# Expert groups of an attention and mixture-of-experts layer: opening products of two experts in a row, then closing products of two

## What is computed

```
x: (32, 256, 128) f32           # 8192 tokens of 128 channels
x = layernorm(x + attention(x)) # 16 heads of 8
# mixture of experts on the result xf, 8192 x 128
scores = sigmoid(xf @ gate_w.T)
sel    = top_k(scores + expert_bias, 2)
for e in range(8):              # each token goes to two experts
    h     = silu((s*xf) @ w1[e].T) * ((s*xf) @ w3[e].T)
    out_r = h @ w2[e].T         # kept where expert e was chosen
shared = silu(xf @ sw1.T) * (xf @ sw3.T) @ sw2.T
x = layernorm(x + shared + s * out_r)
```

## Time and profile before

| | |
|---|---|
| median of 3 runs | 772.97 us (772.28 to 772.98) |
| profiled execution, whole time | 773.07 us |
| profiled execution, span of the records | 771.3 us |
| attention phase, up to the first opening product | 426.6 us |
| expert phase, first opening product to the end | 344.7 us |
| busy in the span: PE, PEld, DVE, ACT, POOL | 744.4, 532.1, 635.0, 520.8, 501.8 us |

### The profile page before, as it was taken

How to read it: one execution, slowest core, us unless ns; L and a number is a source line. 1 busy time by engine, 2 the same in 40 slices (tenths; PEclk the granted TensorE clock), 3 DMA queues, 4 the chain that set the end, 5 groups by cost and what they waited for, 6 DMA issues and landing times.

```text
span 771.3 us, 20493 instructions
## 1 busy us (share of the span) xinstructions
PE 744.4 (97%) x7004; PEld 532.1 (69%) x7004; DVE 635.0 (82%) x1358; ACT 520.8 (68%) x1067; POOL 501.8 (65%) x715
## 2 busy tenths in 40 slices
PE   4899999999999999999998899999999999999996
PEld 2255656566566565665554688888888888888886
DVE  7789999999999999999998557888667666666676
ACT  2178899998889898898888546445455454545442
POOL 5546788887787877878634556566656556555564
PEclk9999999999999999999999999999999999999999
DMA  4747766676565665656610645555554655454540
GB/s 115 200 134 189 183 169 178 187 185 176 151 164 166 174 176 160 157 167 162 172 38 23 196 121 111 121 132 128 141 123 126 130 130 127 125 128 120 125 111 28
DMA packets 202336, 108.92 MB, mean 141 GB/s; under 512 B 10504, under 2 KB 202248, under 8 KB 202248
## 3 DMA queue, kind: packets, MB, share of 16 engines
q1 hardware_dynamic: 199792, 105.75, 53.0%
q10 hardware_dynamic: 2456, 2.05, 1.0%
HBM read 73.41 MB, written 33.82 MB: 139 GB/s over the span
## 4 chain that ended last, share of the span: by engine, by line
PE 92%; DVE 4%; DMA 2%; issue 1%; ACT 1%; SPq 0%; POOL 0%; POOLq 0%; DVEq 0%; ACTq 0%
PE bank L952 16%; PE bank L762 16%; PE bank L734 11%; PE bank L769 9%; PE bank L770 8%; PE bank L771 8%; PE bank L747 8%; PE bank L851 3%; PE bank L825 2%; PE bank L873 2%; PE bank L905 1%; PE bank L880 1%; DVE negmax L1101 1%; PE bank L790 1%; PE bank L889 1%
## 5 line engine op out<-in xcount | busy, mean ns | idle before, releaser
L1101 DVE TENSOR_REDUCE negmax<-bank 128x2 f32<-128x512 f32 x512 | 322.9, 678 | 18.5 <-PE bank L747 16.1
L598 ACT ACTIVATE probs<-bank 128x512 f32<-128x512 f32 x512 | 294.2, 613 | 48.2 <-PE bank L734 44.3
L708 ACT ACTIVATE q_stack<-k_stack 128x512 f32<-128x512 f32 x128 | 80.8, 631 | 152.2 <-DVE k_stack L1160 152.1
L747 PE MATMUL bank<-k_stack,q_stack 48*128 48x256 bf16 x1024 | 163.8, 281 | 3.7 <-DVE negmax L1101 2.3
L734 PE MATMUL bank<-q_stack,k_stack 50*128 50x256 bf16 x1024 | 157.9, 275 | 0.8 <-ACT probs L598 0.7
L1160 DVE TENSOR_TENSOR k_stack<-bank,probs 128x512 f32<-128x512 f32 x128 | 88.2, 689 | 73.2 <-PE bank L771 67.2
L762 PE MATMUL bank<-probs,v_aug 128*32 128x256 f32 x2048 | 137.9, 387 | 0.2 <-ACT attT L609 0.2
L769 PE MATMUL bank<-x_hi,hi_w 128*128 128x512 f32 x288 | 126.4, 439 | 1.2 <-DVE res L1113 0.5
L734 PEld LDWEIGHTS bank<-q_stack,k_stack 50*128 50x128 bf16 x1024 | 75.8, 95 | 73.0 <-issue 35.5
L770 PE MATMUL bank<-x_hi,lo_w 128*128 128x512 f32 x288 | 114.0, 396 | 0.0
L771 PE MATMUL bank<-x_lo,hi_w 128*128 128x512 f32 x288 | 113.6, 394 | 0.0
(11 more groups left out here) (128 smaller groups left out, 1205.9 us busy)
## 6 DMA issues: line engine op xcount, KB each, us to landing
probs<-route_dram SPq DMA_DIRECT2D x128, 256.0 KB, 5.0
q_stack<-q_parts_dram SPq DMA_DIRECT2D x64, 192.0 KB, 3.3
k_stack<-k_parts_dram SPq DMA_DIRECT2D x64, 192.0 KB, 4.2
k_parts_dram<-k_parts SPq DMA_DIRECT2D x32, 192.0 KB, 2.2
q_parts_dram<-q_parts SPq DMA_DIRECT2D x32, 192.0 KB, 2.1
xT_sb<-xT SPq DMA_DIRECT2D x32, 128.0 KB, 2.2
k_parts_dram<-k_parts SPq DMA_DIRECT2D x32, 128.0 KB, 2.0
q_parts_dram<-q_parts SPq DMA_DIRECT2D x32, 128.0 KB, 2.1
```

What stands on the lines that cost most here:

```text
L598: nc.scalar.activation(probs[h][:], score_ps[bank(b, h)][:].rearrange("p (j t) -> p j t", j=NT), ACT.Exp).then_inc(exp_done, 1)
L708: nc.scalar.activation(act[n % DEPTH], gated[n % DEPTH] if n else up1_ps[0][:], ACT.Silu).then_inc(act_set, 1)
L747: mm = pe.matmul(max_ps[bank(b, h)][:, i * T:(i + 1) * T], q_stack[b.ring][first:last, h // 2, i * P:(i + 1) * P], k_stack[b.ring][first:l ...
L1101: nc.vector.tensor_reduce(negmax[b.ring % 2][:, :, column], max_ps[bank(b, head)][:].rearrange("p (i s) -> p i s", i=NT), AX_X, ALU.max, n ...
```

## The change

Line 964 called one `down` after each `up`. Now, with k = 9g + n counting the experts over all groups (whose parity is that of `r * NE + n`, r = g % 2), nothing follows an `up` of even k, and after an `up` of odd k two closing products stand in a row, those of experts k - 5 and k - 4:

```
                     up(g, n, r)
...
-                    if n >= LAG or past(g, 1):
-                        down(g, n - LAG, r if n >= LAG else 1 - r)
+                    if (r * NE + n) % 2:
+                        for m in (n - 1 - LAG, n - LAG):
+                            if m >= 0 or past(g, 1):
+                                down(g, m, r if m >= 0 else 1 - r)
```

## The result

| | before | after |
|---|---|---|
| median | 772.92 us | 781.05 us |
| lowest to highest, 4 runs each | 772.28 to 772.98 | 780.45 to 781.84 |
| ratio to before, 95% interval | | 1.0107 (1.0094 to 1.0119) |
| profiled execution | 773.07 us, span 771.3 | 781.84 us, span 780.0 |

The changed kernel is 8.1 us slower. The forecast was 779.4, so the direction held and 1.7 us of the loss were missing from the sum. The profiled execution of the changed kernel was the longest of its four, so differences read from the two traces come out some 0.6 larger than that of the medians.

What follows compares the result with a forecast made beforehand. TensorE, busy for all 96 us of the expert-phase window, was taken as the bound. Terms 0 (switches) + 0.24 + 1.56 + 2.07 + 1.20 + 1.05 + 0.27 = 6.4 us on the median of 772.97 gave 779.4; range 776.6 to 782.2.

Steps and rivals of the forecast that it cites:

- What bounds the kernel; the switches: Expert phase: TensorE is the bound; 70 fewer pairs of switches change 0 us, between -0.7 and +0.7.
- rounds of two: Sign on TensorE in odd groups: rounds of two 4.58 to 4.60 us apart; shorter if a switch costs something.
- TensorE's busy time should stay: Sign in the profile after: TensorE's busy time itself stays the same.
- The rival that read a price out of the records' durations: First opening matmul behind each closing product: 0.09 us a pair, 6.3 gain; 773.1 (chance 0.06) or 766.7 (0.05).
- The wait of `hidden(3)`: Even groups: `hidden(3)` waits for expert 0's later closing product, stalling `up(6)` 0.24 us; 1.20 in five plain groups.
- Group 0: First group, behind the attention's last pieces: `up(6)` stalls 0.24 us by the same chain, between 0 and 1.
- The fit of 0.2 us in plain groups: Plain even groups, to `hidden(6)`: 7.79 us needed, 8.02 available, so no further stall at the next group's opening.
- VectorE becomes the bound in plain groups: Rival: VectorE's work 0.6 us longer than 6.45 adds 0.4 in each of five groups; some 783 us, chance 0.14.
- Group 4 to 5, and group 2: Routing work delays `hidden(6)`: stalls of 2.07 us from group 4, and 1.56 from group 2 into group 3.
- Group 15 and the end: `down(15, 0)` waits for VectorE's add, 1.05 us; last closing product waits for GpSimd's scalings, 0.27 us.
- The restart price of 0.16: Any stall of TensorE on VectorE ends 0.16 us after VectorE's end; bounds 0.05 to 0.16.
- The alternative of a weight load slipping ahead: Weight load for `up(6)` passes the wait: each of ten stalls loses some 0.11 us; sum 5.3, time 778.3.

Runs made afterwards that it cites:

- e3b_eps: The changed kernel with the addition of epsilon moved from VectorE to GpSimd, its small constant tile allocated behind all large tiles: 779.00 us.
- e1_apart: The changed kernel with expert 0's closing product in even groups put back right behind the opening products of expert 4: 777.05 us.
- e2_own: The changed kernel with a buffer of its own for the hidden product of expert 0, TensorE's list unchanged: 776.44 us.
- e4_other_parity: The changed kernel with the pairs shifted by one expert, so expert 0's closing product is late in odd groups: 777.31 us.
- e7_all: The changed kernel with expert 0's own buffer, epsilon on GpSimd (tile behind the others) and group 14's last closing product back in its old place: 773.26 us.

## Why the prediction was right, and where it was short

**What bounds the kernel; the switches.** Right. TensorE's round is the sum of its parts, rounds of two came 4.59 us apart as forecast, and the doubled switches confirm it. That TensorE's busy time should stay was wrong by 3.7 us, because its records overlap and cover short stalls. The rival that read a price out of the records' durations (0.09 us a pair) was wrong by its whole amount.

**The wait of `hidden(3)`.** Right in place and size. Group 6 after:

```profile
572.26 1.05 PE L952 MATMUL bank<-w_sb,q_stack 128*128 128x128 f32 x8
573.15 1.06 PE L952 MATMUL bank<-w_sb,k_stack 128*128 128x128 f32 x8
573.42 0.69 DVE L1172 TENSOR_TENSOR q_stack<-bank,q_stack 128x512 f32<-128x512 f32 x1 [2.37 <-PE bank L952]
574.17 0.50 PE L769 MATMUL bank<-x_hi,hi_w 128*128 128x512 f32 x1
...
574.51 0.39 PE L770 MATMUL bank<-x_hi,lo_w 128*128 128x512 f32 x1
...
578.23 0.69 DVE L1162 TENSOR_TENSOR k_stack<-bank,probs 128x512 f32<-128x512 f32 x1 [0.22 <-DVE stats L1186]
578.37 1.28 POOL L550 TENSOR_TENSOR place<-k_stack,probs 128x512 f32<-128x512 f32 x1 [0.29 <-PE bank L952]
579.24 0.44 DVE L1194 TENSOR_SCALAR var_eps<-mv 128x4 f32<-128x4 f32 x1
579.59 0.68 DVE L1172 TENSOR_TENSOR q_stack<-bank,q_stack 128x512 f32<-128x512 f32 x1
580.40 0.50 PE L769 MATMUL bank<-x_hi,hi_w 128*128 128x512 f32 x1
```

`hidden(3)` starts 1.16 after expert 0's closing product, as in the earlier trace rows, and waited 2.37 for it instead of 0.97 (1.4 longer, as the closing product came 1.40 later; the prediction's list of signs had said about 2). It ends at 574.11, and the first record of `up(6)` stands at 574.17, the second at 574.51. Without a stall the second would have come at 573.15 + 0.89 + 0.23 = 574.27: the stall of 0.24. Group 0, forecast at the same 0.24, had 0.25 there and 0.15 more at the opening of group 1.

**The fit of 0.2 us in plain groups.** This step failed; its price, four stalls, is a part of the 1.7 us missing. The sum gave `hidden(3)` to the end of `hidden(6)` 6.45 us, taken from group 4; here it is 579.59 + 0.68 - 573.42 = 6.85. Two pieces make up the 0.40, some 0.2 each. `weigh(7)` starts 1.09 after the statistics (578.23, from 577.14) where group 4 has 0.91; this piece was in group 6 before as well, and I had left it unplaced. The other is the addition of epsilon, 0.44 instead of 0.17, ending with GpSimd's product. Against a fit of 0.23 that leaves a stall of 0.17. The rest of the 0.24 is the restart, which at these four openings in the loop took 0.23 to 0.24 after VectorE's end instead of 0.16; why, no row shows. In group 14, which is outside the loop and lacks the first piece, there was no stall although the second was there. So both were needed to exceed 0.2, and removing one (e3b_eps) removed the stalls. The rival "VectorE becomes the bound in plain groups" named this place; it came in four groups at 0.24, where the rival had five at 0.4.

The experiments also corrected where this chain begins. In e1_apart and e2_own, `hidden(3)` is on time and the stall is there all the same. In an even group the opening products of experts 6, 7 and 8 now have one pair of closing products among them, 3 x 1.40 + 2 x 0.89 = 6.0 us until the next group's first, instead of 6.9. VectorE's work with the statistics in it has to fit into that.

**Group 4 to 5, and group 2.** Both were right to 0.1 us in the changed kernel. The account behind them was too simple for group 4. With `hidden(3)` freed, 1.17 of 2.08 stayed, and with the epsilon moved too 1.03. VectorE simply has more work in groups 3 and 4 than the squeezed order gives it time for; some of the routing's instructions with two inputs in SBUF are themselves held by GpSimd (line 1064 takes 1.40 us in the changed kernel's trace, 0.42 in that of e4_other_parity, where GpSimd doesn't hold it). That is not new with the change, though: the same instruction, line 1062 there, took 1.40 in the kernel before too. I did not move the routing to test that, so this part is read from the trace and not shown by an experiment.

**Group 3 into 4, 0.98.** Missing from the prediction, which looked for chains only behind a late closing product, and group 3 is odd. The chain is VectorE's unbroken work in group 3, in which one addition took 1.17 instead of 0.17; with the addition on GpSimd (e3b_eps) the stall was gone.

**Group 15 and the end.** Right. The last closing product of group 14, VectorE's add, the first of group 15:

```profile
757.97 1.05 PE L952 MATMUL bank<-w_sb,place 128*128 128x128 f32 x8
...
759.05 0.69 DVE L1183 TENSOR_TENSOR place<-bank,place 128x512 f32<-128x512 f32 x1 [1.70 <-PE bank L952]
...
759.85 1.13 PE L952 MATMUL bank<-w_sb,q_stack 128*128 128x128 f32 x8 [0.83 <-DVE place L1183]
```

1.08 and 0.69, against 1.09 and 0.69 in the earlier trace rows. e7_all, with the two apart, has no stall there.

**The restart price of 0.16.** It held for the stalls at opening products that follow a `hidden`, from group 2 on (0.15 to 0.16), except for the four in the loop named above, at 0.23 to 0.24. The alternative of a weight load slipping ahead, with 5.3 us in all, did not come true.

## What to carry to other kernels

Where the busiest engine runs almost without gaps, compare the length of a round with its parts measured alone before hoping for a gain from grouping: here they agreed, so the best case was zero. Grouping work on that engine made everybody else's supply come in bursts here, and the price was set where the longest chain of another engine met the shortest interval, not by the averages (VectorE was busy for 65.5 of 96 us). If a grouping is wanted all the same, first look for buffers that are read directly by the moved work and give them one more copy: that alone made the changed kernel 4.9 us faster.

## What the hardware showed beside this

**VectorE's small additions wait for GpSimd.** The traces of before, after, e1_apart, e2_own and e4_other_parity hold 75 instances of the epsilon addition (line 1192 in the kernel before). 37 of them took longer than 0.17 us, from 0.42 to 1.18; each had started inside a product of GpSimd and ended 0.02 to 0.03 us after it. The other 38 took 0.17, and GpSimd was idle when they started or had at most 0.14 us left of an operation. The routing's `tensor_tensor` instructions with both inputs in SBUF ended 0.28 after GpSimd's product in the same way, while `weigh`, `hidden` and the residual add, with one input in PSUM, kept 0.67 to 0.69 beside it, as `tensor_reduce` kept 0.41. The Trainium skill, page SBUF — State Buffer, section Who interferes with whom, says that a `tensor_scalar` in a two-port mode and GpSimd lock each other out of a shared port pair for a whole instruction, and that a VectorE instruction with two SBUF inputs contends with a GpSimd instruction that reads SBUF. One with at most one SBUF input outside those modes doesn't, it says, nor does `tensor_reduce`. The traces agree with it on every one of these forms; in which mode the addition ran no row shows.

**A stall can hide in the busy time.** TensorE's windows say 96.00 of 96.00 us with a stall of 0.22 to 0.25 in each of groups 8 to 11, since the record before it reaches past the next one's start. The waits of the weight loads and the distance between starts show it.
